# First pass written out turn by turn, with one attention chain per tile, Newton steps on GpSimd and unread matmuls ahead of data waits

## The chip, the cores and the metric

One core of one Trainium2 chip runs the whole program. TensorE (PE in the profile), VectorE (DVE), ScalarE (ACT), GpSimd (POOL) and SyncE (SP, which issues the DMAs) each run their own list of instructions in order and wait for one another by semaphores. The metric is the time of one execution in microseconds, as the median of several runs. Beside the runs there is one profiled execution, with a trace of every instruction.

## The reference

The program computes two transformer-like layers on 16 images of 16x16 tokens with 96 channels. The change touches only the first half of the first layer:

```
xr = roll(x, (-4, -4)); 4 windows of 8x8 tokens per image, 12 heads of 8 channels
qkv = layernorm(x) @ qkv_w.T + qkv_b
qn, kn = q / max(|q|, 1e-12), k / max(|k|, 1e-12)      # per head
attn = softmax(qn kn' * scale + bias + mask)           # 64x64 per window and head
x1 = x + roll back((attn v) @ proj_w.T + proj_b)
y1 = layernorm(x1) @ sign(W1).T + b1                   # and its largest value, for a quantizer
```

The second half of that layer (quantized y1, Gelu, W2) and the whole second layer (an offset convolution, bilinear sampling, attention over 256 tokens, four experts) follow in later passes, which the change leaves alone.

## The kernel before

**Tiles.** An image is two tiles of 128 tokens; each tile holds two windows. The first pass (its functions end in `_a`) handles one image per *turn* and works on four images at once. `BEHIND_A` says how many turns a part lags: `project_a` (p: load, normalize, qkv, the sums of squares and their inverse roots) works on image j in turn j, `split_a` (r: scale q and k and split them into bf16 pieces in `stack`) on j-1, `attend_a` (a) on j-2 and `finish_a` (f: divide, project, add, normalize, y1) on j-3. `ORDER_A` is the order in which each engine's list goes through the stages of these parts within a turn. `run_pass` writes out turns 1 to 3 and 17 to 19 and puts turns 4 to 16 in a hardware loop.

**The attention chain of an image.** Each 32-bit q and k is cut into three bf16 pieces, so `stack` holds 64 columns per head. POOL's `split` makes most of the pieces (L527 to L536), ACT's `copies` the rest (L1021, L1022). PE turns `stack` around through PSUM (`turn`, L1236), ACT brings it to `stackt` (L1028), PE forms the scores, DVE takes the negative maximum per row (`nm`, L772) and writes it as three bf16 pieces back into `stack` (L713 to L716). PE turns the query side once more (q2t), ACT copies, PE forms the transposed scores with the maximum already subtracted, ACT takes the exponential (L1068), DVE multiplies by the exponential of the bias (`prob`, L779), PE multiplies by the values, and ACT copies the result to `ot` (L1074). Tile 0 uses PSUM banks 2 and 3, tile 1 banks 4 and 5; at every step the two tiles stand side by side in the list, and the product with the values needs banks 2 and 3 for both.

**Roots.** `project_a` on DVE sums the squares (`ss`, L739), guesses the inverse root by an integer shift (L742 to L744) and improves it by three Newton rounds of three instructions (L746 to L748) on 128x48 numbers in `rn` and `rh`. In the next turn `split_a` scales it (L757) and multiplies (L761, `qk`).

**Input.** SP loads an image into `xin` once the last one is normalized, and DVE copies it to `kept(i)` (L731) for the residual.

## Time and profile before

| | us |
|---|---|
| median of 3 runs | 1107.44 |
| lowest and highest | 1101.46, 1107.94 |
| the profiled execution's own time | 1109.34 |
| its span, first to last instruction | 1107.2 |
| setup, until the first image is read | 0 to 51 |
| first pass, 19 turns | 51 to 371 |
| second pass (quantize, Gelu, W2) | 371 to 402 |
| third pass (second layer) | 402 to 1107 |

An instruction's row gives its start, its duration and, in brackets, how long its engine had been idle and what ended that. A share of busy time is a mean over passes with different limits, so the first pass is to be read by itself. PEclk is the granted clock of TensorE as a share of 2.4 GHz: 1.00 is 2.4 GHz and 0.50 is 1.2 GHz.

### The profile page before, as it was taken

What the parts mean: (1) busy time and instruction counts of PE and PEld (TensorE: products, weight loads), DVE (VectorE), ACT (ScalarE), POOL (GpSimd) and SP (SyncE); (2) the same over time, 40 slices, a digit from 0 to 9 for tenths busy, and PEclk for the clock granted to TensorE, in tenths of its full rate; (3) what the DMA queues carried; (4) which work ended last, traced back from release to release, by engine and by line L of the source; (5) the groups of instructions that cost most, each with busy time, mean ns of one, the idle gap of its engine ahead of it and who ended that gap; (6) DMA issues with size and microseconds to landing.
All of it is one profiled execution on the core that took longest, in us unless ns stands there. A gap on an engine that the chain in (4) does not pass through costs nothing.

```text
span 1107.2 us, 26046 instructions
## 1 busy us (share of the span) xinstructions
PE 864.4 (78%) x9126; PEld 592.1 (53%) x9126; DVE 686.0 (62%) x2245; ACT 583.5 (53%) x1241; POOL 228.0 (21%) x396
## 2 busy tenths in 40 slices
PE   0157777777766655578899999999999999998887
PEld 0035555555554334344567557666765666574556
DVE  1257787878785552355485577668757866775543
ACT  0145666666665441135754754675476457546653
POOL 4033333333332000211220220122012112201100
PEclk9987787878686675578798899999989999998999
DMA  3100000000000001333313312321341233123000
GB/s 115 19 10 9 14 7 14 7 14 7 14 4 9 8 7 30 91 76 93 87 32 79 91 45 63 99 72 48 79 99 48 58 93 84 49 66 97 5 4 8
DMA packets 40045, 51.39 MB, mean 46 GB/s; under 512 B 23097, under 2 KB 27242, under 8 KB 40010
## 3 DMA queue, kind: packets, MB, share of 16 engines
q1 hardware_dynamic: 40010, 50.93, 18.3%
q8 instruction: 21, 0.34, 0.1%
q14 instruction: 14, 0.11, 0.0%
HBM read 44.51 MB, written 6.40 MB: 46 GB/s over the span
## 4 chain that ended last, share of the span: by engine, by line
PE 36%; DVE 25%; issue 19%; ACT 9%; DMA 5%; POOL 3%; SPq 2%; DVEq 1%; ACTq 0%; POOLq 0%
PE ps L1231 31%; DVE nm L904 4%; PE ps L1236 3%; DMA haty<-hat_scratch 3%; DVE prob L779 3%; ACT prob L1190 2%; DVE haty L887 2%; DVE acc L974 1%; DVE b_xn L704 1%; SPq L362 1%; POOL srstd L511 1%; POOL prstd L511 1%; PE ps L1519 1%; ACT prob L1068 1%; ACT stack L1021 1%
## 5 line engine op out<-in xcount | busy, mean ns | idle before, releaser
L1231 PE MATMUL ps<-stackt 53*64 53x64 bf16 (+3 forms) x2304 | 136.6, 243 | 48.9 <-ACT prob L1190 21.7
L1028 ACT COPY stackt<-ps 128x768 bf16<-128x768 bf16 x192 | 144.1, 806 | 56.0 <-PE ps L1236 55.9
L904 DVE TENSOR_REDUCE nm<-ps 128x2 f32<-128x512 f32 x192 | 123.2, 683 | 35.0 <-PE ps L1231 34.7
L887 DVE TENSOR_TENSOR haty<-haty,hatx 128x512 f32<-128x512 f32 x96 | 64.2, 686 | 122.5 <-DMA haty<-hat_scratch 121.6
L1215 ACT ACTIVATE hb<-ps 128x512 f32<-128x512 f32 (+1 forms) x128 | 62.9, 492 | 145.7 <-PE ps L1231 144.6
L1231 PEld LDWEIGHTS ps<-stackt 53*64 53x64 bf16 (+3 forms) x2304 | 52.8, 118 | 143.1 <-ACT prob L1190 70.5
L1236 PE MATMUL ps<-identb,stack 128*128 128x128 bf16 x1152 | 91.9, 236 | 38.3 <-DVE stack L716 20.1
L1231 PE MATMUL ps<-b_xnt,we 128*128 128x256 f32 x384 | 112.2, 401 | 4.0 <-ACT hb L1215 3.8
L511 POOL TENSOR_TENSOR prstd<-pveps,neghalf 128x2 f32<-128x2 f32 x48 | 33.7, 701 | 370.9 <-DVE pveps L699 364.1
L1190 ACT ACTIVATE prob<-ps 128x512 f32<-128x512 f32 x192 | 104.8, 602 | 8.3 <-PE ps L1231 7.1
L1236 PEld LDWEIGHTS ps<-identb,stack 128*128 128x128 bf16 x1152 | 76.9, 106 | 53.9 <-DVE stack L716 28.0
L1231 PE MATMUL ps<-we,hb 128*128 128x96 f32 x768 | 97.2, 276 | 0.5 <-ACT hb L1215 0.5
L1231 PEld LDWEIGHTS ps<-we,hb 128*128 128x128 f32 x768 | 92.6, 192 | 5.0 <-ACT hb L1215 3.8
L1231 PE MATMUL ps<-prob,va 64*32 64x64 f32 (+1 forms) x2304 | 93.3, 306 | 1.6 <-DVE prob L779 1.1
L511 POOL TENSOR_TENSOR srstd<-sveps,neghalf 128x2 f32<-128x2 f32 x32 | 22.7, 710 | 293.4 <-DVE sveps L699 293.4
L1231 PE MATMUL ps<-wconv,qpad 128*128 128x96 f32 x576 | 79.5, 298 | 3.0 <-ACT y1all L1126 2.9
L1231 PEld LDWEIGHTS ps<-wconv,qpad 128*128 128x128 f32 x576 | 74.8, 211 | 7.3 <-ACT qpad L1125 3.8
L1231 PEld LDWEIGHTS ps<-b_xnt,we 128*128 128x128 f32 x384 | 63.0, 191 | 26.1 <-issue 11.1
L779 DVE TENSOR_TENSOR prob<-prob,expbias 128x768 f32<-128x768 f32 x32 | 34.5, 1121 | 35.6 <-ACT prob L1068 35.6
L532 POOL TENSOR_TENSOR stack<-res,stack 128x192 bf16<-128x192 f32 x64 | 54.2, 867 | 2.6
L1231 PEld LDWEIGHTS ps<-prob,va 64*32 64x32 f32 (+1 forms) x2304 | 35.1, 113 | 32.4 <-issue 30.6
L1231 PE MATMUL ps<-perm_in,f_xn 128*96 128x128 f32 x64 | 18.1, 436 | 36.8 <-DVE f_xn L704 36.8
(220 smaller groups left out, 1493.5 us busy)
## 6 DMA issues: line engine op xcount, KB each, us to landing
haty<-hat_scratch SPq DMA_DIRECT2D x64, 384.0 KB
hatx<-hat_scratch SPq DMA_DIRECT2D x32, 384.0 KB
hat_scratch<-hat SPq DMA_DIRECT2D x32, 96.0 KB
xraw<-x_scratch SPq DMA_DIRECT2D x17, 96.0 KB, 15.9
out<-acc SPq DMA_DIRECT2D x16, 96.0 KB, 16.5
we<-in_we SPq DMA_DIRECT2D x1, 768.0 KB
xin<-in_x SPq DMA_DIRECT2D x16, 48.0 KB, 1.8
xin<-in_x SPq DMA_DIRECT2D x32, 24.0 KB, 2.0
```

What stands on the lines that cost most here:

```text
L362: sp.dma_start(t[:], A[name]).then_inc(weights_in, 16)
L511: g.tensor_tensor(n["rstd"][:], n["veps"][:], neghalf[:, 0:TILES], ALU.pow).then_inc(S(ready), 1)
L532: own.mark(g.tensor_tensor(st[:, half[x], HD * k:HD * k + HD], rs[:, half[x]], st[:, half[x], HD:2 * HD], ALU.subtract))
L704: ins = v.tensor_scalar(dst[:, t, :], srcs[t], n["mv"][:, t, 0:1], n["rstd"][:, t:t + 1], ALU.subtract, ALU.mult)
L779: v.tensor_tensor(tile_probs(t), tile_probs(t), expbias[:].rearrange("p a b c -> p (a b c)"), ALU.mult).then_inc(S("a_prob"), 1)
L887: v.tensor_tensor(haty[:, :, g, :], haty[:, :, g, :], x, ALU.mult).then_inc(S("c_mul"), 1)
L904: v.tensor_reduce(nm[:, t, a, 2 * pq:2 * pq + 2], ps[:, 2 + a, :].rearrange("p (b n) -> p b n", n=TOK), AX.X, ALU.max, negate=True).then_i ...
L1028: return a.copy(stackt[:, x, :, P * t:P * t + P], bank_bf(bank))
L1190: a.activation(prob[:, u % 4].rearrange("p b n -> p (b n)"), ps[:, 4 + u % 2, :], ACT.Exp, scale=float(HD) ** -0.5).then_inc(S("c_exp"), 1)
L1215: a.activation(hb[:, e % 2].rearrange("p m n -> p (m n)")[:, 2 * TOK * k:2 * TOK * k + n_], ps[:, 6, 0:n_], ACT.Gelu).then_inc(S("c_h"), 1)
L1231: return m.matmul(o, l, r, start=start, stop=stop)
L1236: ins = m.transpose(bank_bf(bank)[:, b, :], stack[:, x, t].rearrange("p h c -> p (h c)")[:, P * b:P * b + P], identb[:])
```

## The change

All of it lies in the first pass.

1. **Written out.** `run_straight` writes out all 19 turns; there is no hardware loop, and image numbers are constants.
2. **A chain per tile.** `attend_a` becomes two parts, a (tile 0, signals `lo_`) and b (tile 1, `hi_`), with signals of their own. The product with the values uses the tile's own two banks, so does the copy to `ot` (one instruction per tile instead of one per bank). `ORDER_A` interleaves the stages of a and b anew.
3. **Two stacks.** Odd images use `stack`, even ones a view of `hatx`, which is otherwise used only in the third pass. The split of an image no longer waits until the image before has turned its queries again.
4. **Newton on GpSimd.** After the guess DVE multiplies the sums by -0.5 (one instruction more); POOL does three rounds of four instructions on 128x48 numbers, each waiting for the one before, and signals `root`.
5. **Merged.** The two scalings by `lscale` become one; the division of the two tiles (two reciprocals, two products) becomes one of each, after both tiles are turned.
6. **Input.** Images are loaded straight into `kept(i)`, two ahead; the copy L731 goes.
7. **Unread matmuls.** `warm(bank, n)` issues n matmuls of 128x512 bf16 elements whose result is overwritten: per image 4 before the layernorm's turn, 2 before each tile's `turn`, 4 before the turn of `ot`. Each group stands behind the wait for its bank and ahead of the wait for its data.
8. Setup: POOL clears the second stack and writes its mask columns (six instructions more).

```diff
-ORDER_A = "apfaffapfrarpfapr"
+ORDER_A = "apbafbaffabpfrbarrfppb"
-BEHIND_A = dict(p=0, r=1, a=2, f=3)
+HALVES = ("lo_", "hi_")
+BEHIND_A = dict(p=0, r=1, a=2, b=2, f=3)
+        def stack_a(i):
+            return stacks[(i - 1) % 2]
+        def run_straight(eng, order, behind, **parts):
+            last = max(behind.values())
+            for j in range(1, IMAGES + last + 1):
+                turn_of(order, {c: p(j - behind[c]) for c, p in parts.items() if 1 <= j - behind[c] <= IMAGES})
@@ SP @@
+            def load_x(i):
+                for rows_, t, part in shifted(i):
+                    sp.dma_start(kept(i)[part, t, :], A["x"][rows_, :]).then_inc(x_loads[(i - 1) % 2], 16)
+            load_x(1)
+            load_x(2)
             def project_a(i):
+                if i + 2 <= IMAGES:
+                    w("xn", 1)
+                    load_x(i + 2)
@@ POOL, project_a @@
+                w("ss", 1)
+                for k in range(3):
+                    own.link(g.tensor_tensor(half, root, root, ALU.mult))
+                    own.link(g.tensor_tensor(half, half, sums, ALU.mult))
+                    own.link(g.tensor_scalar(half, half, 1.5, None, ALU.add))
+                    ins = g.tensor_tensor(root, half, root, ALU.mult)
+                    if k < 2:
+                        own.link(ins)
+                ins.then_inc(S("a_root"), 1)
@@ DVE, project_a @@
-                v.tensor_copy(kept(i), xin[:])
-                for _ in range(3):
-                    own.link(v.scalar_tensor_tensor(half, root, -0.5, root, ALU.mult, ALU.mult))
-                    own.link(v.tensor_tensor(half, half, sums, ALU.mult))
-                    own.link(v.scalar_tensor_tensor(root, half, 1.5, root, ALU.add, ALU.mult))
+                w("root", 0)
+                v.tensor_scalar(sums, sums, -0.5, None, ALU.mult).then_inc(S("a_ss"), 1)
@@ DVE, split_a @@
+                w("root", 1)
+                own.link(v.tensor_tensor(rn[:, :, 0, :], rn[:, :, 0, :],
+                                         lscale[:, :].rearrange("p (a h) -> p a h", a=1).to_broadcast([P, TILES, HEADS]), ALU.mult))
@@ DVE, finish_a @@
+                w("otr", 2)
+                o = ps[:, 6:8, 0:384].rearrange("p t (h c) -> p t h c", c=32)
+                own.link(v.reciprocal(rec[:], o[:, :, :, HD]))
+                v.tensor_tensor(on[:].rearrange("p t (h c) -> p t h c", c=HD), o[:, :, :, 0:HD],
+                                rec[:].to_broadcast([P, TILES, HEADS, HD]), ALU.mult).then_inc(S("a_on"), 1)
@@ PE @@
+            def warm(bank, n):
+                for _ in range(n):
+                    mm(ps[:, bank, :], onesb[:], bias3[:].rearrange("p h t n -> p (h t n)")[:, 0:512])
@@ PE, project_a @@
                 w("qkv_sb", 0)
+                warm(0, 4)
                 w("xn", 1)
@@ PE @@
+            def attend_a(t):
+                def half(i):
+                    w = waits(pe, HALVES[t], i)
+                    w("ot", 0)
+                    warm(2 + 2 * t, 2)
+                    waits(pe, "a_", i)("split", 1)
+                    waits(pe, "a_", i)("copies", 1)
+                    turn(stack_a(i), 2 + 2 * t, 0, t).then_inc(S(HALVES[t] + "qt"), 1)
+                    turn(stack_a(i), 3 + 2 * t, 1, t).then_inc(S(HALVES[t] + "kt"), 1)
@@ PE, finish_a @@
                 w("y1_sb", 0)
+                warm(6, 4)
                 for t in range(TILES):
+                    waits(pe, HALVES[t], i)("ot", 1)
```

**The order on TensorE at the start of a full turn.** `turn` is L1236 before and L1281 after; the added matmuls read `bias` and `onesb`. Before:

```order
L1236 MATMUL ps<-identb,stack 128x128 [waits a_ot]
L1236 MATMUL ps<-identb,stack 128x128 x23
L283 REGISTER_ALU
L1337 MATMUL ps<-ident,ot 128x128 [waits a_ot,a_y1_sb]
L1337 MATMUL ps<-ident,ot 128x128 x5
L283 ISA
L1231 MATMUL ps<-stackt 64x64 [waits a_qt_sb,a_kt_sb]
L1231 MATMUL ps<-stackt 64x64 x23
L283 REGISTER_ALU
L1231 MATMUL ps<-stackt 64x64 [waits a_qt_sb,a_kt_sb]
L1231 MATMUL ps<-stackt 64x64 x23
```

With the change:

```order
L1276 MATMUL ps<-bias,onesb 128x512 [waits lo_ot]
L1276 MATMUL ps<-bias,onesb 128x512
L1281 MATMUL ps<-identb,stack 128x128 [waits a_copies,a_split]
L1281 MATMUL ps<-identb,stack 128x128 x11
L1276 MATMUL ps<-bias,onesb 128x512 [waits hi_ot]
L1276 MATMUL ps<-bias,onesb 128x512
L1281 MATMUL ps<-identb,stack 128x128 [waits a_copies,a_split]
L1281 MATMUL ps<-identb,stack 128x128 x11
L1276 MATMUL ps<-stackt 64x64 [waits lo_qt_sb,lo_kt_sb]
L1276 MATMUL ps<-stackt 64x64 x23
L1276 MATMUL ps<-bias,onesb 128x512 [waits a_y1_sb]
L1276 MATMUL ps<-bias,onesb 128x512 x3
```

The 24 transposes of an image are now two groups of 12, each with its two unread matmuls ahead, and four more stand between the scores of tile 0 and the turn of `ot`; the scores of tile 1 come behind that.

**The order on VectorE from the norms to the first bias product.** L704 is L746 after, L757 is L796, L761 is L801 and L779 is L818. Before:

```order
L704 TENSOR_SCALAR f_xn<-xin,pmv,prstd 128x96 [waits a_rstd]
L704 TENSOR_SCALAR f_xn<-xin,pmv,prstd 128x96
L704 TENSOR_SCALAR b_xn<-xres,smv,srstd 128x96 [waits a_rstd2]
L704 TENSOR_SCALAR b_xn<-xres,smv,srstd 128x96
L338 ISA
L283 ISA
L757 TENSOR_TENSOR rn<-rn,lscale 128x12 [waits a_qkv_sb]
L757 TENSOR_TENSOR rn<-rn,lscale 128x12 [waits dve_sample]
L761 TENSOR_TENSOR qk<-qkv_sb,rn 128x2x96 [waits a_copies,a_split,dve_sample]
L761 TENSOR_TENSOR qk<-qkv_sb,rn 128x2x96
L779 TENSOR_TENSOR prob<-prob,expbias 128x768 [waits a_exp] x2
```

With the change:

```order
L741 TENSOR_SCALAR sveps<-smv 128x2 [waits dve_last]
L818 TENSOR_TENSOR prob<-prob,expbias 128x768 [waits lo_exp]
L746 TENSOR_SCALAR f_xn<-y1all,pmv,prstd 128x96 [waits a_rstd]
L746 TENSOR_SCALAR f_xn<-y1all,pmv,prstd 128x96
L746 TENSOR_SCALAR b_xn<-xres,smv,srstd 128x96 [waits a_rstd2]
L746 TENSOR_SCALAR b_xn<-xres,smv,srstd 128x96
L356 ISA
L796 TENSOR_TENSOR rn<-rn,lscale 128x2x12 [waits a_root,a_qkv_sb]
L801 TENSOR_TENSOR qk<-qkv_sb,rn 128x2x96 [waits a_copies,a_split,dve_sample]
L801 TENSOR_TENSOR qk<-qkv_sb,rn 128x2x96
L818 TENSOR_TENSOR prob<-prob,expbias 128x768 [waits hi_exp]
```

The bias product of tile 0 now stands ahead of both norms and of `qk`, that of tile 1 behind them. What `qk` feeds is the split for the next turn.

## Rows read from the trace of the kernel before

**Rows 1.** Page of the profile, parts 1 and heading: span, then busy time by engine.

```profile
span 1107.2 us, 26046 instructions
...
PE 864.4 (78%) x9126; PEld 592.1 (53%) x9126; DVE 686.0 (62%) x2245; ACT 583.5 (53%) x1241; POOL 228.0 (21%) x396
```

**Rows 2.** Windows: stretch, its length, busy time by engine (x instructions), granted clock, DMA.

```profile
108.40:316.40 208.00, 146.50 (x2882) 113.92 (x2882) 164.20 (x564) 125.19 (x278) 75.03 (x111) 0.78 0.05 10
316.40:371.00 54.60, 35.06 (x684) 25.97 (x682) 30.98 (x97) 29.19 (x60) 13.43 (x20) 0.72 0.04 10
```

**Rows 3.** Timeline of a turn: start, duration, engine, line, operation, then idle before it.

```profile
201.16 0.94 DVE L772 TENSOR_REDUCE nm<-ps 128x12 f32<-128x768 f32 x1
...
206.22 0.57 DVE L704 TENSOR_SCALAR f_xn<-xin,pmv,prstd 128x96 f32<-128x96 f32 x2
...
208.02 0.63 DVE L761 TENSOR_TENSOR qk<-qkv_sb,rn 128x192 f32<-128x192 f32 x2
...
208.84 0.50 POOL L527 CAST stack<-qk 128x384 bf16<-128x384 f32 x1 [1.75 <-DVE qk L761]
209.00 0.35 ACT L1021 CAST stack<-qk 128x192 bf16<-128x192 f32 x1
...
209.15 2.29 PE L1231 MATMUL ps<-wqkv,f_xnt 128*128 128x288 f32 x4
...
210.84 2.18 DVE L779 TENSOR_TENSOR prob<-prob,expbias 128x768 f32<-128x768 f32 x2 [2.19 <-ACT prob L1068]
...
213.78 0.35 POOL L536 CAST stack<-res 128x192 bf16<-128x192 f32 x1
...
214.49 0.87 ACT L1074 COPY ot<-ps 128x384 f32<-128x384 f32 x2
...
215.42 1.51 PE L1236 MATMUL ps<-identb,stack 128*128 128x128 bf16 x24 [0.98 <-ACT ot L1074]
...
215.96 2.91 ACT L1028 COPY stackt<-ps 128x768 bf16<-128x768 bf16 x4 [0.60 <-PE ps L1236]
...
217.56 0.38 PE L1231 MATMUL ps<-stackt 53*64 53x64 bf16 x24
...
219.61 0.95 DVE L772 TENSOR_REDUCE nm<-ps 128x12 f32<-128x768 f32 x1
```

**Rows 4.** Waits from 130 to 310 us: total, times, longest.

```profile
DVE prob L779 <- ACT prob L1068: 21.9, 10, 2.2
```

**Rows 5.** Groups by line and form, 131.7 to 316 us: VectorE, what goes or merges.

```profile
L746 DVE SCALAR_TENSOR_TENSOR rh<-rn 128x48 f32<-128x48 f32 x30 | 6.5, 215 | 1.0
...
L722 DVE TENSOR_TENSOR on<-ps,rec 128x96 f32<-128x96 f32 x20 | 5.1, 257 | 0.7
...
L757 DVE TENSOR_TENSOR rn<-rn,lscale 128x12 f32<-128x12 f32 x20 | 3.4, 168 | 0.3
```

**Rows 6.** The same view: GpSimd instructions.

```profile
L532 POOL TENSOR_TENSOR stack<-res,stack 128x192 bf16<-128x192 f32 x20 | 24.5, 1242 | 0.8
...
L528 POOL TENSOR_TENSOR res<-qk,stack 128x384 f32<-128x384 f32 x10 | 9.1, 912 | 0.8
...
L511 POOL TENSOR_TENSOR prstd<-pveps,neghalf 128x2 f32<-128x2 f32 x10 | 6.9, 690 | 38.0 <-DVE pveps L699 38.0
```

**Rows 7.** Timeline of an early turn: two GpSimd subtractions with no prob product beside them.

```profile
67.36 1.05 POOL L532 TENSOR_TENSOR stack<-res,stack 128x192 bf16<-128x192 f32 x2
```

**Rows 8.** All products by the bias, whole run: shortest, median, longest in ns.

```profile
L779 DVE TENSOR_TENSOR prob<-prob,expbias x32: 951/960/1308, 81.1 to 354.8; 128x768 f32<-128x768 f32 x32
```

**Rows 9.** Windows, TensorE only: stretch, length, busy time (x matmuls), granted clock, DMA.

```profile
206.60:212.10 5.50, 5.26 (x61) 0.50 0.15 31
217.60:222.60 5.00, 2.56 (x62) 1.00 0.00 0
222.60:228.60 6.00, 4.13 (x62) 0.50 0.11 25
```

**Rows 10.** Groups by form from 405 us on: the nearest matmul to the added ones.

```profile
L1231 PE MATMUL ps<-bias,onesb 128*128 128x384 bf16 x32 | 10.5, 327 | 0.1
```

More of the change, by code:

```diff
@@ L353, in build_program @@
         DSETUP = 28
[L354 to L355 removed]
+        PZERO = 16
+        PSETUP = PZERO + 11
         @block.sync
@@ L396, in split_a @@
                     yield
-            def attend_a(i):
-                for _ in range(ORDER_A.count("a")):
-                    yield
+            def attend_a(t):
+                def half(i):
+                    for _ in range(5):
+                        yield
+                return half
             def finish_a(i):
@@ L486, in _ @@
             setup(g.memset(neghalf[:], -0.5))
-            setup(g.memset(stack[:], 0.0))
+            for st in stacks:
+                setup(g.memset(st, 0.0))
             setup(g.memset(va[:], 0.0))
@@ L550, in split_a, with attend_a, half @@
                 w("qk", 2)
-                w("q2t", 0)
+                for h in HALVES:
+                    if i > 2:
+                        waits(pool, h, i)("q2t", -1)
                 settle(pool, "pool")
-                yield from split(own, qk[:].rearrange("p a t h c -> p (a t h) c"), S("a_split"))
+                yield from split(own, stack_a(i), qk[:].rearrange("p a t h c -> p (a t h) c"), S("a_split"))
                 yield
-            def attend_a(i):
-                values_in(waits(pool, "a_", i), v_new[:], S("a_va"))
-                for _ in range(5):
-                    yield
+            def attend_a(t):
+                def half(i):
+                    w = waits(pool, HALVES[t], i)
+                    w("pv", 0)
+                    waits(pool, "a_", i)("v", 1)
+                    settle(pool, "pool")
+                    g.tensor_copy(va[:, t, :, 0:HD], v_new[:, t]).then_inc(S(HALVES[t] + "va"), 1)
+                    for _ in range(5):
+                        yield
+                return half
             def finish_a(i):
@@ L613, in split_c @@
                 settle(pool, "pool")
-                yield from split(own, queries_keys(i), S("c_split"))
+                yield from split(own, stack[:], queries_keys(i), S("c_split"))
                 yield
@@ L1014, in _, with copies @@
             act.wait_ge(setup_pool, PSETUP)
-            def copies(src, ready):
+            def copies(stack, src, ready):
                 for x, b in ((0, 3), (1, 2)):
@@ L1280, in split_a, with attend_a, half @@
                     yield
-            def attend_a(i):
-                w = waits(pe, "a_", i)
-                w("split", 1)
-                w("copies", 1)
-                w("ot", 0)
-                for t in range(TILES):
-                    turn(2 + 2 * t, 0, t).then_inc(S("a_qt"), 1)
-                    turn(3 + 2 * t, 1, t).then_inc(S("a_kt"), 1)
-                yield
-                for t in range(TILES):
-                    w("qt_sb", t + 1)
-                    w("kt_sb", t + 1)
+            def attend_a(t):
+                def half(i):
+                    w = waits(pe, HALVES[t], i)
[5 more added lines that the diff above has]
+                    turn(stack_a(i), 3 + 2 * t, 1, t).then_inc(S(HALVES[t] + "kt"), 1)
+                    yield
+                    w("qt_sb", 1)
+                    w("kt_sb", 1)
                     settle(pe, "pe")
```

207 lines of the change are left out of this document (100 added, 107 removed).

## The prediction, made before the change was run

> **What bounds the kernel now.** I begin at the top of the page: in a span of 1107.2 us no engine is busy throughout, TensorE 78% and VectorE 62% [rows 1]. The shares mix passes, and the change is in the first pass alone, so I read windows of that pass: in its full turns VectorE is busy 164.2 of 208.0 us, 79%, TensorE 146.5 at a mean clock of 0.78, ScalarE 125.2, GpSimd 75.0 [rows 2]. VectorE leads, but does not fill the time. The timeline shows a turn of 18.45 us, from the reduction at 201.16 to the same one at 219.61 [rows 3]. The one long wait of VectorE in it is for the exponentials, 2.19 us at 210.84; ten turns wait 21.9 us [rows 3, 4]. So a turn is about 16.2 us of VectorE work and its small gaps, and 2.2 us of waiting in the attention chain. Both can shrink, and what remains is whichever circle of waits is longest. Of such turns there are 14 (4 to 17).
>
> **VectorE work.** Nine Newton instructions go, one comes: 8 x 0.24 (0.215 busy plus a gap, [rows 5]) = 1.95 us. The copy into `kept(i)`, one scaling and two of four division instructions go, 0.17 to 0.26 us each by their neighbours [rows 5]; the merged ones are longer by some 0.1, so 0.7 in all. That leaves 16.2 - 2.65 = 13.5 us per turn. It would be the turn only if VectorE never waited.
>
> **The circle that remains.** `qk` of an image is written late in a turn; its split feeds the next turn's transposes, these feed the scores, and VectorE reaches the next `qk` only behind that turn's reductions. Walked with the rows of the old turn, from PE's turn of tile 0:
> - Transposes to the reduction of tile 0. 215.42 to 217.56 is the wait for two ScalarE copies and the start of the scores, then 0.38 for the scores and 0.1 to signal [rows 3]: 2.6 us. Before, the reduction began only at 219.61, since the norm and the division stood ahead; now tile 0 goes first.
> - Reduction to the end of `qk`. 219.61 less the turn is 201.16, and the norm began at 206.22: 5.06. New in between are the merged division, 0.6 (two instructions of 0.26 and a little more, [rows 5]), and tile 0's bias product, 0.95 when undisturbed [rows 8]. From the norm to `qk` 1.80, less one scaling 0.2; `qk` 0.63 [rows 3]. Sum 8.8.
> - End of `qk` to the next transposes. GpSimd starts 0.19 later and took from 208.84 to 214.13, 5.3 us [rows 3], with both bias products beside it. Its two subtractions took 1.24 each there [rows 6], but 1.05 together with no product beside them [rows 7]: 1.4 us of the 5.3 is disturbance. With one product beside it I take half: 4.6, so 4.8 with the start.
>
> That is 2.6 + 8.8 + 4.8 = 16.2. To it I add 0.2 for Newton steps that disturb VectorE (below): **16.4 us per turn**. The bounds of the third leg are 4.1 (undisturbed) and, by ScalarE, 5.4: its casts began at 209.00, 0.35 after `qk`, and `ot` was out at 215.36, 6.35 later, of which one exponential (0.75) is now done earlier; its next copy can start 0.54 behind the transposes [rows 3]. So the turn lies between 15.6 and 17.0.
>
> **What is hidden.** The chain of one tile, about 10 us from transposes to `ot`, now ends before the split does, so the 2.2 us wait for the exponentials goes; what is late next is the split, and VectorE should wait for the scores of tile 0 instead, about 16.4 - 13.5 = 3 us. The second stack lets the split ignore the old image's last transposes. The DMAs keep their number and were never waited for in a full turn. The six extra setup instructions of GpSimd lie before 24 us, the first image is read at 51; if they did not fit they would cost some 3 us once.
>
> **The unread matmuls.** The profile of before has no matmul of 512 bf16 columns. The nearest row is 384 columns, 0.33 us as a mean with its latency [rows 10]; I bound one by 0.2 and 0.45 and take 0.25, so 3 us of TensorE per turn. Six of the twelve precede data that the walk has later than they end: four before the norm (TensorE is free 1 to 2 us there), two before tile 0's transposes, where the product of tile 1 ends about 0.5 us ahead of the split. The two of tile 1 run beside ScalarE's copies. The four before the turn of `ot` delay the scores of tile 1 by 1 us, and VectorE needs these 2.4 us after the scores of tile 0. If any of this cover is gone, a group costs 0.5 to 1 us per turn. What they may return is the clock. From 217.60 to 222.60 it stood at 1.00 while TensorE was busy for 2.56 of 5.0 us, and behind that it was 0.50 for the next 6 us; from 206.60 to 212.10 it was 0.50 too, under 5.26 us of work in 5.5, and the four qkv matmuls took 2.29 us in it [rows 3, 9]. With the gaps filled I expect a mean above 0.9, and qkv near half of 2.29. The walk uses rows of full clock; that part of the gain hangs on this.
>
> **Newton on GpSimd.** Twelve dependent steps of 48 columns. GpSimd's rows are 0.91 us for 384 columns and about 0.53 for 192 undisturbed [rows 6, 7]; going on down gives 0.25, with the gap 0.32, 3.8 us in all. They start about 1.2 us into the next turn, when the sums are ready, and the same queue then has a copy of values (0.35) and the norm's root (0.75 with its gap, [rows 6]) before VectorE wants that root at 2.6 + 5.06 + 0.6 + 0.95 = 9.2. So they may take 6.9 us, 0.57 a step. Below that they cost nothing but disturbance: two three-piece subtractions of VectorE fall in their time, at up to 0.25 each; I took 0.2 of these 0.5.
>
> A rule bears on this. The Trainium skill, page "SBUF — State Buffer", section "Who interferes with whom", says that a VectorE instruction with two SBUF inputs and a GpSimd instruction that reads SBUF exclude each other, and the second waits for the first to end. The trace agrees for the bias product: 0.96 at the median and 1.31 at the longest [rows 8]. By the rule each of the two subtractions would wait out a whole step, 0.5 us a turn in place of 0.2.
>
> **Sum.** 14 turns x (18.45 - 16.4) = 28.7. Turns 18 and 19 are a single chain with little beside it and span most of the last 54.6 us [rows 2]; two tiles side by side should give 1.5 us each, 3 in all. Filling turns 1 to 3 neither gain nor lose, the Newton chain being 1.6 longer against shorter VectorE work: 0, with 1 either way. 1109.3 - 31.7 = 1077.6. That is against the profiled execution, whose 1109.34 lies 1.9 above the median of 1107.44; I leave the difference in and say **1078**.
>
> **The rivals.**
> - *The port rule in full*: the two subtractions wait whole steps and the split's subtractions meet more of VectorE's. 0.3 to 0.6 us a turn more, 1082 to 1086. For it the longest product, against it that most of VectorE's work in that time reads PSUM. Chance 0.08.
> - *VectorE becomes the bound*: the split and ScalarE are quicker than the walk, turns of 13.6 to 14.5, 14 x 4.0 to 4.9 less: 1038 to 1052. Against it, the split alone is 3.9 us and the third leg cannot be below 4.1. Chance 0.07.
> - *The clock stays mixed*: matmuls between a norm and the scores keep today's length, 1.1 us for qkv and a few tenths each for the transposes, so turns of 17.6 to 18.4 and 1095 to 1108. For it: some idle time ahead of each norm remains. Chance 0.12.
> - *GpSimd's steps are dear*: the root of the tiny 128x2 tile took 0.69 [rows 6]. If a step costs more than 0.57 with its gap, VectorE's norm waits for GpSimd; above 0.57 + 2.05/12 = 0.74 the kernel is slower than before. At 0.77 (that root's size) the turn is 18.8 and the time 1112; at 0.98 (the row of 384 columns) 21.3 and 1147. Against it: that root is a power, and the columns fell from 384 to 48. Chance 0.05.
> - *The tables don't do what they say*: another wait in the new order, or fetching written-out code, eats the gain: 1098 to 1115. The written-out turns of before (1 to 3, 17 to 19) show no idle time for want of instructions. Chance 0.06.
>
> **Forecast.** The walk itself, 15.6 to 17.2 us a turn, 1065 to 1090, has 0.62. The range 1050 to 1103 takes in the port rule, most of the mixed clock and the edge of the VectorE case, and leaves out about 0.17. A difference of 1% (11 us) is what a measurement of this kernel can tell from none; faster than 1096 are the walk, the port rule, the VectorE case and 0.03 of the mixed clock, 0.80; slower than 1118 are the GpSimd case and 0.03 for the unnamed wait being larger than I set it, 0.08; the rest is 0.12.
>
> **What would show it.** Right: full turns of 16 to 17 us; PEclk above 0.9; VectorE's longest wait now the reduction of tile 0 for TensorE; GpSimd's split at 4 to 5 us; Newton steps near 0.3 us; no wait of the norm for GpSimd. Wrong: clock near 0.8, the norm waiting for `prstd`, or TensorE starting transposes without idle time before them, which would mean that the unread matmuls are in the way.

## The result, and the profile of the changed kernel

The changed kernel takes **1076.05 us** at the median (1071.99 to 1078.14, 4 runs), the kernel before 1107.69 in the same session: a ratio of 0.9716, 95% interval 0.9674 to 0.9757. Forecast were 1078, in a range of 1050 to 1103. The profiled execution took 1075.66. Two executions were longer at a lower clock and are left out of the medians below: one of the kernel with one stack, by 27 us, and one of the kernel without the matmuls ahead of the transposes, by 30 us, which is its profiled one and of which only the first pass is read.

The page, its head and the busy line; against [rows 1] VectorE has lost 41 us and GpSimd has gained 58.

```profile
span 1073.9 us, 25725 instructions
...
PE 870.6 (81%) x9272; PEld 581.1 (54%) x9318; DVE 645.4 (60%) x2053; ACT 581.2 (54%) x1241; POOL 286.4 (27%) x610
```

Windows of the changed kernel (stretch, length, busy time of PE, PEld, VectorE, ScalarE and GpSimd with instructions, granted clock, DMA): the full turns, and the end of the first pass.

```profile
106.00:316.00 210.00, 171.40 (x3496) 122.15 (x3533) 153.53 (x483) 143.61 (x323) 129.21 (x289) 0.99 0.06 13
316.00:345.00 29.00, 14.64 (x164) 9.69 (x163) 11.86 (x33) 9.53 (x17) 2.41 (x3) 0.63 0.05 11
```

The clock of the full turns went from 0.78 [rows 2] to 0.99; that of the drain is still mixed. One full turn, from the reduction of tile 0 to the next one (start, duration, engine, line, operation, then the idle time before it):

```profile
199.22 0.96 DVE L812 TENSOR_REDUCE nm<-ps 128x12 f32<-128x768 f32 x1 [0.53 <-PE ps L1276]
...
202.03 0.29 POOL L574 TENSOR_TENSOR rn<-rh,rn 128x48 f32<-128x48 f32 x1
...
203.79 0.35 DVE L836 TENSOR_TENSOR xres<-y1all,ps 128x192 f32<-128x192 f32 x1
...
204.99 0.95 DVE L818 TENSOR_TENSOR prob<-prob,expbias 128x768 f32<-128x768 f32 x1
205.16 1.33 POOL L539 TENSOR_TENSOR srstd<-sveps,neghalf 128x2 f32<-128x2 f32 x1 [1.74 <-DVE sveps L741]
...
206.53 0.57 DVE L746 TENSOR_SCALAR b_xn<-xres,smv,srstd 128x96 f32<-128x96 f32 x2
...
207.22 0.63 DVE L801 TENSOR_TENSOR qk<-qkv_sb,rn 128x192 f32<-128x192 f32 x2
...
208.05 0.50 POOL L549 CAST hatx<-qk 128x384 bf16<-128x384 f32 x1 [1.56 <-DVE qk L801]
...
209.87 1.13 PE L1276 MATMUL ps<-wqkv,f_xnt 128*128 128x288 f32 x4
209.99 0.96 DVE L818 TENSOR_TENSOR prob<-prob,expbias 128x768 f32<-128x768 f32 x1 [2.13 <-ACT prob L1114]
...
212.21 0.35 POOL L558 CAST hatx<-res 128x192 bf16<-128x192 f32 x1
...
212.62 0.84 PE L1281 MATMUL ps<-identb,hatx 128*128 128x128 bf16 x12 [0.32 <-POOL hatx L558]
...
215.20 0.96 DVE L812 TENSOR_REDUCE nm<-ps 128x12 f32<-128x768 f32 x1 [0.54 <-PE ps L1276]
```

The turn is 15.98 us where it was 18.45 [rows 3]; the mean of ten full turns (from the reduction of image 3 to that of image 13) is 16.01 and was 18.48. It splits at two marks that every kernel below has: the end of `qk` and the start of the next transposes. Here: reduction to the end of `qk` 207.85 - 199.22 = 8.63, from there to the transposes 4.77, transposes to the reduction 2.58. The last GpSimd cast ends at 212.56 and the transposes start at 212.62: the split is what they wait for. The `qkv` matmuls took 1.13 us, half of the old 2.29.

Groups by form, 103 to 279 us of the changed kernel: the new GpSimd steps, and one root in two surroundings (times in ns).

```profile
L539 POOL TENSOR_TENSOR srstd<-sveps,neghalf 128x2 f32<-128x2 f32 x11 | 14.6, 1327 | 19.6 <-DVE sveps L741 19.6
L573 POOL TENSOR_SCALAR rh<-rh 128x48 f32<-128x48 f32 x33 | 11.0, 332 | 2.9
...
L571 POOL TENSOR_TENSOR rh<-rn 128x48 f32<-128x48 f32 x33 | 8.8, 267 | 15.7 <-DVE ss L787 14.0
L539 POOL TENSOR_TENSOR prstd<-pveps,neghalf 128x2 f32<-128x2 f32 x11 | 7.9, 723 | 0.0
```

Waits of the changed kernel, 130 to 300 us (total, times, longest):

```profile
DVE prob L818 <- ACT prob L1114: 23.5, 11, 2.1
...
DVE nm L812 <- PE ps L1276: 6.8, 11, 1.5
...
DVE gm L844 <- ACT y1all L1136: 5.5, 11, 0.5
```

The wait for the exponentials did not go. It is as long as in [rows 4], but it is now that of tile 1, and it ends nothing: `qk` stands before it, and the split runs during it. VectorE's 3.2 us of waiting per turn are spread over three places.

**Balance.** From the first reduction of image 1 to the first of image 16, in fifteen intervals, the old profile takes 272.43 us (73.29 to 345.72), the new one 238.47 (72.69 to 311.16): -34.0. The twelve full turns among them give 30.1, the first interval 2.2, and the last two, which were only 17.36 and 16.35 us long before, 1.7. From there to the end of the first pass it took 25.08 and takes 27.43: **+2.35**. With -0.6 ahead of it the first pass ends 32.2 us earlier (370.8 to 338.6). The other passes are 1.1 shorter, within the scatter of the runs. The drain, on TensorE of the changed kernel:

```profile
318.98 0.66 PE L1402 MATMUL ps<-ident,b_xn 128*96 128x128 f32 x2 [2.72 <-DVE b_xn L746]
...
320.94 2.91 PE L1276 MATMUL ps<-b_xnt,w1s 128*128 128x256 f32 x6
...
332.28 0.66 PE L1402 MATMUL ps<-ident,b_xn 128*96 128x128 f32 x2 [2.83 <-DVE b_xn L746]
333.40 2.93 PE L1276 MATMUL ps<-b_xnt,w1s 128*128 128x256 f32 x6 [0.46 <-ACT b_xnt L1132]
```

```profile
317.00:323.00 6.00, 4.02 (x79) 3.07 (x80) 2.30 (x4) 2.04 (x4) 1.32 (x1) 0.50 0.07 16
330.50:339.00 8.50, 3.59 (x8) 2.08 (x8) 2.01 (x7) 2.86 (x5) 0.79 (x2) 0.50 0.10 24
```

The four unread matmuls ahead of the norm belong to the projection of a later image, so the drain has none there. TensorE idles 2.8 us before each `b_xn`, the clock is at 0.50 behind it, and the six matmuls of `y1` take 2.9 us; in a full turn they took 1.56. But the drain of the kernel before was no better: its last two `y1` took 2.75 and 2.93, the last one here:

```profile
365.60 2.93 PE L1231 MATMUL ps<-b_xnt,w1s 128*128 128x256 f32 x6 [0.46 <-ACT b_xnt L1087]
```

So the low clock of `y1` is not what makes the +2.35. It is mostly the order. The mark itself has moved: the reduction of image 16 stood behind the division and now stands ahead of it, and from that reduction to `xres` it is 4.46 us where it was 3.50. From `xres` to `b_xn` it is 2.74 for 2.09, with tile 0's bias product in between, and from `b_xn` to `y1` 2.58 for 2.00, as a product of probabilities and values now stands between them in TensorE's list. Behind that nothing differs but 0.17. Counted from `y1` of image 14 to the end, the old kernel takes 33.84 us (from 336.96) and the new one 33.76 (from 304.83): the drain lost nothing and gained nothing.

### The profile page after: what moved, and what is told of

Its sections match the earlier page's. It is cut to its first block, busy times and chain, and to the rows that moved or that the text cites. A ratio compares the mean times of both kernels' runs of the same rounds, so it can differ in the third digit from the quotient of the medians.

```text
span 1073.9 us, 25725 instructions
## 1 busy us (share of the span) xinstructions
PE 870.6 (81%) x9272; PEld 581.1 (54%) x9318; DVE 645.4 (60%) x2053; ACT 581.2 (54%) x1241; POOL 286.4 (27%) x610
## 3 DMA queue, kind: packets, MB, share of 16 engines
q1 hardware_dynamic: 40010, 50.93, 18.4%
## 4 chain that ended last, share of the span: by engine, by line
PE 39%; DVE 18%; issue 16%; ACT 10%; POOL 9%; DMA 5%; SPq 2%; DVEq 0%; ACTq 0%; POOLq 0%
PE ps L1276 33%; DVE nm L946 4%; PE ps L1281 4%; DMA haty<-hat_scratch 3%; ACT prob L1235 2%; DVE haty L929 2%; POOL srstd L539 2%; ACT y1all L1136 1%; DVE acc L1016 1%; POOL rh L573 1%; SPq L380 1%; DVE b_xn L746 1%; ACT stackt L1073 1%; POOL rh L572 1%; PE ps L1569 1%
## 5 line engine op out<-in xcount | busy, mean ns | idle before, releaser
L1276 PEld LDWEIGHTS ps<-stackt 53*64 53x64 bf16 (+3 forms) x2304 | 49.8, 105 | 131.4 <-ACT prob L1235 70.1
L539 POOL TENSOR_TENSOR srstd<-sveps,neghalf 128x2 f32<-128x2 f32 x32 | 31.7, 990 | 243.8 <-DVE sveps L741 243.8
L1281 PE MATMUL ps<-identb,stack 128*128 128x128 bf16 x864 | 65.1, 226 | 8.4 <-DVE stack L758 4.6
L1276 PE MATMUL ps<-bias,onesb 128*128 128x512 bf16 (+1 forms) x178 | 54.6, 384 | 16.4 <-DMA cbias<-bpart 9.2
L1281 PEld LDWEIGHTS ps<-identb,stack 128*128 128x128 bf16 x864 | 54.8, 102 | 23.7 <-DVE stack L758 9.1
L818 DVE TENSOR_TENSOR prob<-prob,expbias 128x768 f32<-128x768 f32 x32 | 30.9, 966 | 35.5 <-ACT prob L1114 35.5
L1177 ACT ACTIVATE tn<-tn 128x192 f32<-128x192 f32 x16 | 5.8, 363 | 72.2 <-DVE tn L909 72.2
## 6 DMA issues: line engine op xcount, KB each, us to landing
out<-acc SPq DMA_DIRECT2D x16, 96.0 KB, 16.4
```

Of the source, the lines that this page charges most:

```text
L539: g.tensor_tensor(n["rstd"][:], n["veps"][:], neghalf[:, 0:TILES], ALU.pow).then_inc(S(ready), 1)
L818: v.tensor_tensor(tile_probs(t), tile_probs(t), expbias[:].rearrange("p a b c -> p (a b c)"), ALU.mult).then_inc(S(HALVES[t] + "prob"), 1)
L1276: return m.matmul(o, l, r, start=start, stop=stop)
L1281: ins = m.transpose(bank_bf(bank)[:, b, :], stack[:, x, t].rearrange("p h c -> p (h c)")[:, P * b:P * b + P], identb[:])
```

## The experiments

Three sets of four kernels. Each set has its own runs of the kernel before (1107.68, 1106.22, 1107.57 us), and ratios are to those; that of the change is to its own 1107.69.

**First set: which part does it.** The changed kernel without the unread matmuls:

```diff
             def warm(bank, n):
-                for _ in range(n):
+                for _ in range(0):
```

> The changed kernel without its twelve unread matmuls per image, all else kept. Theory A (they hold the clock, and the clock shortens the matmuls that stand in the circle of waits): the granted clock in full turns falls from 1.00 to 0.75-0.85, the qkv matmuls go back from 1.1 to about 2.2 us, the turn goes from 15.98 us to 16.9-17.6, total 1090-1100 us. Theory B (the clock does not matter here, since ScalarE, GpSimd and VectorE make up the circle): turn 15.8-16.1, total 1073-1078.

With the matmuls, but with Newton's steps back on VectorE:

```diff
-                w("root", 0)
-                v.tensor_scalar(sums, sums, -0.5, None, ALU.mult).then_inc(S("a_ss"), 1)
+                for _ in range(3):
+                    own.link(v.scalar_tensor_tensor(half, root, -0.5, root, ALU.mult, ALU.mult))
+                    own.link(v.tensor_tensor(half, half, sums, ALU.mult))
+                    own.link(v.scalar_tensor_tensor(root, half, 1.5, root, ALU.add, ALU.mult))
```

> The changed kernel with the three Newton rounds back on VectorE (nine instructions, 2.2 us with gaps), unread matmuls kept. Theory A (the circle through GpSimd's split has only 0.5 us of slack for VectorE between the sums of squares and the reduction of tile 0): that reduction starts 1.2-1.6 us later, less 0.3-0.5 us that GpSimd no longer disturbs; turn 16.8-17.3, total 1088-1096. Theory B (moving them was worth nothing, because VectorE waits 3 us per turn anyway): turn 15.6-16.0, total 1071-1077.

With both edits:

> The changed kernel without the unread matmuls and with Newton back on VectorE: what remains is the chain per tile with its order, the second stack, the merged instructions and the written-out turns. If the two effects add up: turn 18-18.5, total 1103-1110, that is no gain over before. If each hides part of the other (VectorE late already, so that slower matmuls fall beside its work): turn 17.2-17.8, total 1094-1101.

The kernel before, with its first pass written out and nothing else:

```diff
+            if parts.keys() == BEHIND_A.keys():
+                for j in range(1, IMAGES + last + 1):
+                    turn(j, lambda n: 1 <= j - n <= IMAGES)
+                return
```

> The kernel before with its 19 turns of the first pass written out instead of a hardware loop, nothing else. Theory A (loop and register instructions lie beside VectorE's work or cost 0.1-0.3 us a turn): 1103-1107. Theory B (writing out is a main part of the gain): under 1100. Theory C (fetching straight code costs): over 1112.

Measured, with the ratio's interval. The turn, its three legs and the range of the turns are of ten full turns (images 3 to 13), legs and turn as means; the last column is where the first pass ends in the trace. All in us:

```
kernel                          median   ratio (95% interval)      turn   range          to qk end  to transposes  to reduction  pass ends
before                          1107.69                            18.48  18.43 to 18.59   7.49       6.56           4.43         370.80
before, written out             1098.27  0.9923 (0.9897-0.9949)    18.03  17.96 to 18.27   7.15       6.70           4.18         364.70
new order, neither part         1132.01  1.0221 (1.0192-1.0251)    20.43  20.12 to 20.88   9.43       5.87           5.12         395.14
new order, matmuls only         1098.65  0.9921 (0.9892-0.9950)    18.12  17.46 to 18.86   8.92       4.88           4.32         365.09
new order, Newton moved only    1088.65  0.9834 (0.9790-0.9879)    16.99  16.74 to 17.82   8.74       5.22           3.03         352.48
the change                      1076.05  0.9716 (0.9674-0.9757)    16.01  15.97 to 16.33   8.67       4.76           2.58         338.59
```

All three times were missed. Taking out the matmuls costs 12.6 us, a little less than theory A had, at the clock that it had (0.82); but the `qkv` matmuls did not go back, they take 1.13 us here too. Moving Newton's steps back costs 22.6 us, more than its theory A had, and doing both costs 56.0, far more than either theory. Writing out came out as theory B. The matmuls are worth 12.6 us where Newton's steps are on GpSimd and 33.4 where they are on VectorE; moving the steps is worth 22.6 with the matmuls and 43.4 without. Each part does some of the other's work. With Newton's steps on VectorE the matmuls don't hold the clock throughout, it is 0.89, and the long ones of those turns are turns with matmuls at the low clock. The turn without either shows how (first VectorE's waits in a turn of that kernel, then its window, and that of the kernel with only the Newton move):

```profile
193.90 0.35 DVE L826 TENSOR_TENSOR xres<-y1all,ps 128x192 f32<-128x192 f32 x1 [1.53 <-PE ps L1266]
...
200.65 1.01 DVE L808 TENSOR_TENSOR prob<-prob,expbias 128x768 f32<-128x768 f32 x1 [2.69 <-ACT prob L1104]
...
203.49 0.95 DVE L834 TENSOR_REDUCE gm<-y1all 128x1 f32<-128x768 f32 x1 [1.83 <-ACT y1all L1126]
```

```profile
106.00:316.00 210.00, 146.34 (x2618) 113.69 (x2618) 139.65 (x477) 112.90 (x252) 69.01 (x112) 0.70 0.05 11
```

```profile
106.00:316.00 210.00, 156.55 (x3140) 120.61 (x3140) 146.11 (x468) 136.28 (x304) 126.75 (x285) 0.82 0.06 13
```

Newton's steps on VectorE stand before the reduction of tile 0, 1.7 us longer than TensorE needs (the last leg, 4.32 against 2.58). TensorE has nothing to do there; without the unread matmuls its clock drops, the projection takes 1.17 instead of 0.69 us, `xres` waits 1.53 us for it, and `y1`, 2.68 instead of 1.56, holds up the maximum of `y1all` and, by TensorE's queue, the transposes. The mean of 20.43 is 18.12 plus 0.51, 0.99 and 0.80 in the three legs; I read all three as the low clock's, by way of `y1` above all, and the run with the matmuls added supports it, though no run separates the legs. So the new order alone, tiles apart and divisions merged, is not a gain: it is 34 us slower than the old order written out. It puts TensorE into a circle that was VectorE's, and in these runs it paid as far as VectorE's work between transposes and reduction was small and the clock stayed up.

Writing out, which I had priced at nothing, is worth 9.4 us by the medians; in the profiled runs the first pass is 6.1 us shorter (370.8 to 364.7). The edit does not touch the later passes; the ratio's interval, 5.6 to 11.4 us, takes in 6.1, so I put the rest down to scatter. Where it is, in the waits of the kernel before (130 to 300 us) and then at one place of either kernel's turn:

```profile
DVE xres L794 <- issue: 2.0, 10, 0.2
```

```profile
204.57 0.21 DVE L716 TENSOR_TENSOR stack<-nmr,stack 128x12 bf16<-128x12 f32 x1
...
204.98 0.35 DVE L794 TENSOR_TENSOR xres<-y1all,ps 128x192 f32<-128x192 f32 x1 [0.20 <-issue]
```

```profile
200.54 0.21 DVE L720 TENSOR_TENSOR stack<-nmr,stack 128x12 bf16<-128x12 f32 x1
200.64 0.35 DVE L798 TENSOR_TENSOR xres<-y1all,ps 128x192 f32<-128x192 f32 x1
```

In the loop, the instruction that reaches a slice of `y1all` by the image's number starts 0.41 us behind its predecessor, written out 0.10. The maximum of `y1all` and the division start 0.1 earlier each. Of these 0.5 us the turn keeps 0.45 (means of 18.48 and 18.03). Whether the address or the loop's own register instructions cost it, no run separates; and one turn of the written-out kernel, from 251.17, has the late start too, 0.45.

**Second set.** The twelve unread matmuls in the kernel before, at the same places of its order:

```diff
+                warm(0, 4)
                 w("xn", 1)
...
+                w("ot", 0)
+                warm(2, 2)
+                warm(4, 2)
                 w("split", 1)
...
+                warm(6, 4)
                 for t in range(TILES):
```

> The kernel before with the twelve unread matmuls per image of the first pass alone (four ahead of the norm's wait, two and two ahead of the turns of the next image, four ahead of the turn of ot). Theory A (the clock matters only where TensorE is in the circle of waits; the old circle is VectorE's 16.2 us of work plus 2.2 us for the exponentials, with little of TensorE in it): the granted clock rises above 0.9, a turn falls by at most 0.5 us, 1100 to 1104 us. Theory B (the clock by itself is worth what the matmuls returned in the changed kernel without them, 12.6 us, or more, since here it starts from 0.78): 1088 to 1096 us. Theory C (they are only worth something once the gaps are short): the clock stays under 0.85 and the time is 1107 or more.

1114.31 us (1111.22 to 1115.85), 1.0068 (1.0045 to 1.0091): slower by under 1%, but beyond the interval, at a clock of 0.90 in the full turns. Theory C has the sign without its reason, since the clock did rise. A turn of it, TensorE:

```profile
217.22 1.04 PE L1231 MATMUL ps<-bias,onesb 128*128 128x512 bf16 x4 [0.95 <-ACT ot L1074]
...
218.09 1.50 PE L1236 MATMUL ps<-identb,stack 128*128 128x128 bf16 x24
```

Here the copies of `ot` end last, not the split, so the four matmuls stand between that copy and the transposes, 0.87 us. I took this for the circle: the legs are 7.50, 7.06 and 3.90, in all 18.46, as before. It is not: in this turn VectorE works from its bias product at 213.22 to the reduction at 221.99 without a gap, and waits for no transposes. Most turns are of this kind (18.4 to 18.5). In the longest, 19.5 to 19.8, the clock fell, and the division waits for the turn of `ot`, which comes behind both groups of four in TensorE's list; one of them on VectorE:

```profile
240.62 0.23 DVE L721 RECIPROCAL rec<-ps 128x12 f32<-128x12 f32 x1 [1.19 <-PE ps L1346]
```

The same kernel without those four:

```diff
-                warm(2, 2)
-                warm(4, 2)
```

> The kernel before with eight unread matmuls per image: the twelve of the run before less the four ahead of the turns of the next image, which stood 0.87 us long between the end of the copy of ot and the transposes. Theory A (those four stood in the circle and took back what the clock gave): turns of 17.6 to 18.0 us and 1095 to 1101 us. Theory B (without them the clock falls behind the transposes as in the kernel before, and the other eight earn nothing): turns of 18.4, 1105 to 1110 us.

1110.34 us (1107.24 to 1117.32), 1.0033 (1.0013 to 1.0054): both theories missed. Its turns alternate between 18.36 and 19.20. The short kind is what the old order has at a full clock, 0.1 less than before: the clock is worth nearly nothing to it. Without the four the transposes of such a turn start 0.77 us earlier after `qk` (6.29 for 7.06), but the turn is only 0.1 shorter, and the mean of ten turns is 18.78 us against 18.72 with them. So the four are not what took back the gain; there was hardly any. In the long kind the transposes and the group ahead of the turn of `ot` ran at the low clock (2.72 and 1.48 us for 1.50 and 1.04):

```profile
216.79 2.72 PE L1236 MATMUL ps<-identb,stack 128*128 128x128 bf16 x24 [1.14 <-ACT ot L1074]
...
219.31 1.48 PE L1231 MATMUL ps<-bias,onesb 128*128 128x512 bf16 x4
...
221.15 0.23 DVE L721 RECIPROCAL rec<-ps 128x12 f32<-128x12 f32 x1 [0.70 <-PE ps L1344]
```

They delay the transposes of `ot`, the division waits 0.70 us for them, and in the old order the division stands before the reduction, in the circle. In the new order it stands behind it. That is the cover the same group has there.

Unread matmuls in the drain of the changed kernel:

```diff
+                if i == IMAGES:
+                    warm(0, 3)
                 w("on", 1)
...
+                if i > IMAGES - 3:
+                    warm(0, 10)
                 w("xn2", 1)
...
+                if i == IMAGES:
+                    warm(0, 2)
                 w("x2t_sb", 1)
```

> The changed kernel with unread matmuls in the drain of the first pass as well, where the projection's group of four is absent: ten ahead of the wait for the gated y1 in the last three images, and five more about the last image's on. Theory A (the drain became 2.35 us longer because TensorE fell to 0.50 in it and the two y1 products took 2.9 us each): y1 takes 1.5 to 1.6 us in the last two images, the first pass ends 3 to 5 us earlier than 338.6, and the time is 1071 to 1073 us. Theory B (the drain is longer by the contended root and the new order): y1 is shorter, but the first pass ends within 1 us of 338.6 and the time stays at 1075 to 1077.

1071.15 us (1069.33 to 1076.41), 0.9684 (0.9657 to 0.9711). The first pass ends at 335.3, 3.3 us earlier. TensorE in the drain:

```profile
316.44 2.32 PE L1276 MATMUL ps<-bias,onesb 128*128 128x512 bf16 x10
319.32 0.42 PE L1406 MATMUL ps<-ident,b_xn 128*96 128x128 f32 x2 [0.56 <-DVE b_xn L746]
...
320.64 1.56 PE L1276 MATMUL ps<-b_xnt,w1s 128*128 128x256 f32 x6
```

The numbers are those of theory A: `y1` takes 1.56 us and the drain 23.84 us for 27.43. The interval overlaps that of the change, so the gain rests on the trace. It doesn't show theory A's reason for the 2.35 us: the drain of the kernel before ran at the low clock too. From the reduction of image 16 to `y1` of image 15 it takes 9.14 us here, at a clock of 1.00, and took 7.59 there. What it shows is that 3.3 us of the first pass hang on the clock of its drain. Ten matmuls took 2.32 us, 0.23 each.

Tile 0's bias product moved behind `qk` on VectorE:

```diff
-            run_straight(dve, ORDER_A, BEHIND_A, ...)
+            run_straight(dve, "apbafbaffbpfrabarrfppb", BEHIND_A, ...)
```

> The changed kernel with tile 0's bias product on VectorE moved from ahead of the norm to behind qk. It takes 1.1 to 1.2 us out of the leg from the reduction to qk (the product and part of the wait for GpSimd's root, which then runs at 0.7 instead of 1.33 us) and sets the product beside GpSimd's split, where the second product was already. Theory A (the port rule prices it: two products beside the split lengthen it by about what the leg gains): turn 15.7 to 16.3 us, 1073 to 1080 us. Theory B (no contention worth naming): turn 15.2 to 15.4, 1065 to 1069 us. Theory C (the attention chain of tile 0, held back by 1.5 us, becomes the circle): turn 16.8 or more, 1088 or more.

1074.78 us (1069.38 to 1077.76), 0.9691 (0.9658 to 0.9723). Nine turns have 15.8 to 16.2 us, with legs of 7.90, 5.34 and 2.58: the first is 0.73 shorter than in the change, the second 0.57 longer. Groups of this kernel, 103 to 279 us:

```profile
L539 POOL TENSOR_TENSOR srstd<-sveps,neghalf 128x2 f32<-128x2 f32 x11 | 7.7, 697 | 15.6 <-DVE sveps L741 15.6
L551 POOL CAST hatx<-res 128x384 bf16<-128x384 f32 x6 | 7.0, 1161 | 0.4
...
L549 POOL CAST hatx<-qk 128x384 bf16<-128x384 f32 x6 | 6.2, 1032 | 9.3 <-DVE qk L801 9.3
```

The root is back at 0.70 us, and two casts that took 0.50 take 1.03 and 1.16; the two subtractions behind them, 1.66 in the change, take 1.06 in all, since the other product has moved off them. This is theory A: a VectorE product of two SBUF operands cost GpSimd 0.53 to 0.66 us wherever it landed. The Trainium skill, "SBUF — State Buffer", "Who interferes with whom", says the second of such a pair waits for the first to end. In the turn shown above that gives for the root 205.94 - 205.16 + 0.72 = 1.50 us, and 1.33 was measured; the rule holds but for some 0.15. Five more turns had 17.2 us. In every turn TensorE now idles 0.93 us ahead of the product of probabilities and values, which waits for the moved bias product; in those five the clock is low behind it. TensorE in one of them:

```profile
160.90 0.94 PE L1276 MATMUL ps<-prob,va 64*32 64x64 f32 x48 [0.93 <-issue]
161.77 2.83 PE L1276 MATMUL ps<-b_xnt,w1s 128*128 128x256 f32 x6
```

`y1` took 2.83 us and not 1.56, and the turn was 1.4 longer. Three unread matmuls in that gap, and those of the drain:

```diff
+                    if t == 0:
+                        w("exp", 1)
+                        warm(2, 3)
                     w("prob", 1)
```

> The changed kernel with tile 0's bias product behind qk, three unread matmuls ahead of the wait for that product (where TensorE was idle for 0.93 us and the clock fell in six turns of the earlier run), and the unread matmuls of the drain. Theory A (the clock is all that cost those turns 1.4 us each): every full turn 15.8 us, the first pass ends at 332.5 to 334.5, 1066 to 1071 us. Theory B (the three delay the product of probabilities and values and with it y1, the maximum of y1 and the next reduction): turns of 16.0 to 16.5, 1071 to 1079 us.

1069.30 us (1065.47 to 1069.56), **0.9652 (0.9625 to 0.9679)**, the lowest of the study, though its interval touches that of the change and overlaps that of the drain's matmuls alone. All full turns have 15.83 to 15.96 us (and one 16.20), the first pass ends at 333.2. Theory A.

One stack instead of two:

```diff
-            return stacks[(i - 1) % 2]
+            return stacks[0]
...
-                    if i > 2:
-                        waits(pool, h, i)("q2t", -1)
+                    waits(pool, h, i)("q2t", 0)
```

> The changed kernel with one stack instead of two: GpSimd and ScalarE wait for tile 1's second transposes of the image before they write the split. Theory A (the second stack is slack: those transposes are over some 4 us before the split starts): 1075 to 1078 us, turn 16.0. Theory B (it was needed, the transposes of tile 1 being held behind the unread matmuls): turn 16.3 or more, 1080 or more.

1073.22 us, 0.9702 (0.9668 to 0.9735), turns of 15.97: theory A, the second stack is worth nothing here, though the median is a little under its range.

**Third set, the rest.** One Newton step instead of three:

```diff
-                for k in range(3):
+                for k in range(1):
```

> The changed kernel with one Newton step (four instructions of GpSimd) instead of three; the root of the sums is then coarser, nothing else is left out. Theory A (the twelve instructions are hidden but for what they disturb: the last eight run beside VectorE's short instructions between the two reductions, which are 0.3 us longer in all than in the kernel before): turn 15.6 to 15.8 us, 1070 to 1074 us. Theory B (something waits for the root or for GpSimd): turn 15.4 or less, under 1069. Theory C (entirely hidden): 15.98 and 1074 to 1077.

1072.61 us (1071.67 to 1072.94), 0.9689 (0.9660 to 0.9718). The turn is 15.87, 0.11 less, between theories A and C; the time is in the range of A. Fourteen turns make 1.5 us; 2.6 come from the first image, whose root nothing covers (its first reduction is at 70.07 instead of 72.69; in the other kernels with the steps on GpSimd it is at 71.66 to 73.74). In the trace the first pass ends 4.2 us earlier.

Without the unread matmuls ahead of each tile's transposes:

```diff
-                    warm(2 + 2 * t, 2)
```

> The changed kernel without the two and two unread matmuls ahead of the transposes of each tile, the other eight kept. Theory A (in this kernel they are over before the split is, so they cost nothing, and they keep the clock through the wait for the split): without them the clock falls in some turns, turn 16.2 to 17, 1079 to 1089 us. Theory B (eight are enough for the clock): turn 15.98, 1074 to 1077 us. Theory C (they delay the transposes here too): turn under 15.8, under 1072 us.

1073.69 us, 0.9713 (0.9681 to 0.9745), turns of 15.97 at a clock of 0.98. Theory B: these four of the twelve do nothing in the changed kernel, neither good nor harm, but for one turn of 17.15 us, from 184.07, in which `y1` took 2.73 us at the low clock. The change has a longer turn at the same image, 16.33, since `xres` starts 0.35 late there, and its `y1` stays at 1.56. One turn can't tell whether the four keep the clock in such a case.

## Why the forecast held, step by step

**The circle** was the right picture. Forecast 2.6, 8.8 and 4.8 and 0.2 of disturbance, 16.4; measured 2.58, 8.63 and 4.77, 15.98. The first and third leg are exact to 0.03. The second was 9.0 with the disturbance and is 8.63: 0.24 of the 0.4 is the norm. `b_xn` followed `f_xn` by 0.91 us in the old loop, as it waited 0.34 for GpSimd's root; now the bias product stands ahead, the root is ready in time, and it is 0.67. I had carried the 0.91 over in the 1.80. The rest is 0.08 of the product and 0.09 of the work between the reduction and the norm.

**A step that failed: writing out is worth nothing.** I had looked for idle time for want of instructions in the few written-out turns, which is what could make it dear, and not at the looped ones for what it saves. A row of the trace of before had it, 0.2 us ten times, put down to "issue". In the old order it is worth 9.4 us by the medians and 6.1 in the traces of the first pass; what it is worth in the new order no run shows, and there `xres` starts 0.29 behind its predecessor, 0.12 less than in the loop.

**The drain failed too.** Forecast -3 from two tiles side by side; measured nothing from `y1` of image 14 on (33.84 and 33.76 us), and +2.35 from the reduction of image 16. Why two tiles side by side gave no 1.5 us each stays open. The low clock of the drain, which I had not priced, costs 3.3 in the new kernel; the last two `y1` of the old one were as long, so I take most of it to have been paid there too, which no run tests.

**The number of turns** was wrong as well. From turn 17 on there is no image to project, and the last two of the fourteen old intervals were 17.36 and 16.35 us, not 18.45. The twelve full ones gave 30.1, where fourteen of 2.05 were to give 28.7. So 34.0 was gained between the reductions against 28.7, and 2.4 lost against 3 gained behind them; the errors cancel, and that the median came within 2 us of the forecast is luck in part.

**VectorE's waits.** The wait for the exponentials stayed at 2.1 us, where I expected it to go and the scores of tile 0 to take its place with 3. I had followed tile 0 only. Tile 1's product now has that wait, off the circle. The total, 3.2 us, was right.

**Unread matmuls.** Price 0.22 to 0.23, in the bounds of 0.2 to 0.45 and near the 0.25 taken; clock 0.99, above the 0.9. `qkv` halved to 1.13, but not through them: it takes 1.13 without them too, at a mean clock of 0.82, and what they shorten is `y1` (1.56 for 2.0 to 2.8 us), behind which tile 1's product of probabilities and values and the next transposes stand in TensorE's list. What I had not seen is that four of them are idle ballast, and that their worth is not a property of them: 33.4, 12.6 and, in two versions of the kernel before, -8.1 and -2.8 us. In the old order TensorE is hardly in the circle, so the clock gave 0.1 us a turn, and whenever the clock did fall the groups stood ahead of a division that the circle needs. In the new order they are beside it.

**Newton on GpSimd.** Forecast 0.32 a step with its gap, 3.8 in all; measured 0.27 to 0.33 with gaps of 0.07 to 0.1, 4.5 in all, well below the 6.9 allowed. Eight of the steps disturb by 0.11 us a turn, less than the 0.2. Where I had not looked, a product did disturb GpSimd: the root of the second norm, 1.33 instead of 0.72, beside tile 0's bias product. `b_xn` starts when it ends, at the head of the chain to `qk`, but `f_xn` had ended only 0.11 us before.

**Rivals.** The mixed clock (1095 to 1108) is the case of the kernel without the matmuls, with a clock of 0.82, and it took 1088.65: the rival was priced too dear, since it let `qkv` keep its old length. The 1098.65 with the steps on VectorE lies in that range for another reason. Of the others, none came up: VectorE still waits 3.2 us a turn, a step of GpSimd takes 0.37 with its gap where 0.57 was allowed, and no new wait was found. Fetching written-out code can't be ruled out for the one late start of `xres`, 0.35 us once in the pass, whose cause stays open.

## What to carry to other kernels

Write down the circle of waits and ask what stands in it, before and after: the same twelve matmuls were worth 33 us, 13 us and less than nothing, by whether TensorE was in the circle or only what they could delay was. Compare two drains by the same instruction of the same image: a mark that the change itself moves within the turn puts a gain in one stretch and a loss in the next. A reordering that is slower alone (here by 34 us) can be the base of the gain; judge it with what it needs. Look at loops for short idle times before instructions whose addresses follow the counter, and give the drain of a pipeline what keeps its full turns fast, in the old kernel as well as in the new one.

## What the runs showed of the hardware that I had not expected

- A GpSimd cast of 128x384 takes 0.50 us alone, and 1.03 to 1.16 beside a VectorE product of two SBUF operands; a root of 128x2 takes 0.70 and 1.33.
- Ten matmuls of 128x512 bf16 took 2.32 us and held the granted clock at 1.00 in a stretch of 3 us in which TensorE had idled 2.72.
- The same gap of 0.93 us in the same place was followed by `y1` at half clock in five full turns and at full clock in eight others.
- In the hardware loop a VectorE instruction whose operand is reached by the loop's counter started 0.31 us later than the same one written out.
- 24 transposes of 128x128 bf16 took 1.50 us at full clock and 2.72 at the low one.
